# Signals of TensorE carried by a drain behind a batch's last product, in the gather passes of a graph network

## The chip, the cores and the metric

The kernel runs on one core of a Trainium2 chip. The metric is the device time in microseconds of one execution without profiler; the median of 3 executions counts. The engines are TensorE (PE; its weight loads are PEld), VectorE (DVE), ScalarE (ACT), GpSimd (POOL) and SyncE (SP), each with an instruction stream of its own; they wait for each other on semaphores alone.

## What is computed

Four layers of a graph network on 6250 nodes of 64 features and 200000 edges sorted by destination. Each layer normalises the nodes (layer norm, then the positive part), works on the edges and adds its result to the nodes. Cut to the edge work:

```python
def layer0(h): # sum of neighbours
    agg = segment_sum(concatenate([h[src], edge_attr_32], axis=1), dst)
    return relu(concatenate([h, agg], axis=1) @ W.T + b)

def layer1(h): # additive attention; V belongs to the destination
    pre = h[src] @ W_q + b_q + h[dst] @ W_k + b_k + edge_attr_32 @ W_e + b_e
    scores = leaky(pre) @ a_w + a_b
    alpha = segment_softmax(scores, dst)
    return segment_sum(alpha * (h[dst] @ W_v + b_v), dst)

def layer2(h): # weighted sum
    return segment_sum(h[src] * (edge_weight_n2 * edge_weight)[:, None], dst)

def layer3(h): # attention with 4 rules, 8 relations
    q = h[dst] @ Wq + bq
    key = h[src] @ Wk1 + rel_emb[edge_type] @ Wk2 + bk
    scores = ((q * key).sum(-1)[:, None] + q @ key_rule.T) / 8
    mean_attn = segment_softmax(scores, dst).mean(axis=1)
    out = segment_sum(h[src] @ W_r[edge_type] * mean_attn[:, None], dst) + bias
    return relu(layer_norm(out))
```

## The kernel before

Edges are taken in 392 batches of 512, four tiles of 128 edges each. Since edges are sorted, the destinations of one batch lie in a window of 128 nodes, and a segment sum over a batch is a product with one-hot rows of the destination's place in the window.

There are four passes over all batches. Three of them gather rows of a table in HBM by source node, with GpSimd's indirect DMA, one for each tile of 128 edges (`gather_stage`, L785):

- **the sum pass** (`sum_sweep`, layer 0) gathers `node_rows`. In one batch of eight the rows are not gathered but made by TensorE, as products of one-hots with the whole node table in SBUF (`look_up`, L1119); VectorE (L1191) and ScalarE (L1089, L1093) build these one-hots. TensorE's stage `sums` (L1111) makes four products, whose signal s_sum frees the gathered rows and lets VectorE add the sum (L1160).
- **the score pass** (`score_sweep`, layer 1) gathers `src_rows`. TensorE's stage `look` makes one product with the edge features (L1480) and twelve with the table of destination rows (L1485), signal s_looked. VectorE joins them with the gathered rows and computes the scores. ScalarE writes them on the diagonals of four matrices (`spread_stage`, L1391), TensorE's stage `spread` brings them into all partitions (L1382), signal s_spread, and VectorE masks (L1529) and takes the maximum. SP's `stream` waits for s_looked to load the next edge features, ScalarE's spread_stage for s_spread to reuse the diagonals.
- **the attention pass** (`attention_sweep`, layer 3) gathers `rel_rows`. TensorE has four stages: `look` (L1663, twelve products, s_looked), `sum_up` (L1689, four fp32 products, s_sum), `find` (L1680, four small products, s_found), `spread` (L1671 in bf16 and L1382 in fp32, s_spread). VectorE takes the maximum (L1714) and the running maximum in three parts (L1723 to L1756), which `find` waits for; ScalarE makes a factor out of it (`shrinks`, L1629), then the diagonals (L1391), which `spread` waits for.

The fourth pass (`kept_sum_sweep`, layer 2) reads back rows that the score pass has spilled to HBM; nothing is gathered in it.

On each engine `pipeline` (L160) lays the stages out, in one order for every step: a stage with lag n handles in step t the batch t - n. TensorE's orders are `sums`, `lookups` in the sum pass, `look` (1), `spread` (6) in the score pass and `look` (1), `sum_up` (5), `find` (3), `spread` (2) in the attention pass. The steps in the middle are a loop over 8 or 16 unrolled steps. `done(eng, sem, b)` waits until a stage has finished batch b, `free(eng, sem, b, ring)` until the batch that had the same ring slot before is done with it. Gathered rows lie in a ring of 8 batches. GpSimd waits before a batch's gathers for the slot: s_sum in the sum and attention passes, s_pre (VectorE) and the spill in the score pass.

Every one of TensorE's stages signals by an increment on its last product:

```python
for g in range(TILES_PER_BATCH):
    last = pe.matmul(summed, weighted[:, b.slot(2), g, :],
                     rows[:, b.slot(ROW_RING), g, D:2 * D + 1],
                     start=(g == 0), stop=(g == TILES_PER_BATCH - 1))
last.then_inc(s_sum, 1)
```

`look` reads the place of the batch's window out of registers (`dst_table`, `Bases.of`), which is register work of TensorE's own instruction stream. A phase ends in barriers (L215, L218, L221), in which each engine has a drain with a semaphore increment.

Of the kernel before, what the change touches and what calls it, by code (L numbers as in the profile page):

```python
# [64 lines left out]
ROW_RING = 8  # L65
# [172 lines left out]
def graph_layers(nc, a, out):  # L238
    ctx = contextlib.ExitStack()
    with ctx:  # L240
# [689 lines left out]
        def sum_sweep(name):  # L930
# [4 lines left out]
            def sweep():  # L935
                with Phase(nc, name) as ph:
# [163 lines left out]
                    @block.tensor  # L1100
                    def _(pe):
                        def sums(b):
                            done(pe, s_onehot, b)
                            if looked_up(b):
                                pe.wait_ge(s_filled, block_of(b))
                            else:
                                rows_landed(pe, s_rows, b)
                            done(pe, s_joined, b)
                            free(pe, s_added, b, 2)
                            for g in range(TILES_PER_BATCH):  # L1110
                                last = pe.matmul(sum_bank(b), sum_rows[:, b.slot(ROW_RING), g, :],  # L1111
                                                 onehots_of(b)[:, g, :],
                                                 start=(g == 0), stop=(g == TILES_PER_BATCH - 1))
                            last.then_inc(s_sum, 1)

                        def look_up(b, hot, j):
                            for g in range(TILES_PER_BATCH):
                                at = g % 2 * PARTS * D
                                last = pe.matmul(look_banks(b)[g // 2][:, at:at + PARTS * D],  # L1119
                                                 hot[:, g * P:(g + 1) * P], node_parts(j),  # L1120
                                                 start=(j == 0 and g % 2 == 0),
                                                 stop=(j == SRC_TILES - 1 and g % 2 == 1))
                            return last

                        def lookups(b):
                            if not has_lookup(b):
                                return
                            if b.slot(LOOK_EVERY) == 0 and not b.early(2 * LOOK_EVERY):
                                pe.wait_ge(s_filled, block_of(b) - 1)
                            by_dve, by_act = list(hots_dve(b)), list(hots_act(b))  # L1130
                            before_dve, before_act = block_of(b) * HOTS_DVE, block_of(b) * HOTS_ACT
                            for n, m in enumerate(by_dve):
                                pe.wait_ge(s_hot_dve, before_dve + m + 1)
                                look_up(b, dve_hots[:, m % 4, :], m).then_inc(s_used_dve, 1)
                                for k in by_act[n // 2:n // 2 + 1] if n % 2 else []:
                                    pe.wait_ge(s_hot_act, before_act + k + 1)
                                    look_up(b, act_hots[:, k % 2, :], HOTS_DVE + k)\
                                        .then_inc(s_used_act, 1)
                            for k in by_act[len(by_dve) // 2:]:
                                pe.wait_ge(s_hot_act, before_act + k + 1)  # L1140
                                look_up(b, act_hots[:, k % 2, :], HOTS_DVE + k).then_inc(s_used_act, 1)
                        pe.wait_ge(s_parts, (PARTS + 1) * len(src_groups))
                        pipeline(pe, [(0, sums), (0, lookups)], unroll=GATHER_UNROLL)
# [262 lines left out]
        def score_sweep(name):  # L1406


            def sweep():
                with Phase(nc, name) as ph:  # L1410
# [61 lines left out]
                    @block.tensor  # L1472
                    def _(pe):
                        def look(b):
                            parts = dst_table(b)
                            done(pe, s_hot, b)
                            free(pe, s_pre, b, RING)
                            landed(pe, s_dma, b, 16)
                            to = banks[b.slot(RING)][:, 0:TILES_PER_BATCH * D]
                            pe.matmul(to, edge_blocks[:, b.slot(RING), :],  # L1480
                                      w1_e[:, :, :].rearrange("p g f -> p (g f)"),
                                      start=True, stop=False)
                            for g in range(TILES_PER_BATCH):
                                for n, part in enumerate(parts):
                                    last = pe.matmul(  # L1485
                                        to[:, g * D:(g + 1) * D],
                                        onehotT[:, b.slot(ONEHOT_RING), g, :], part, start=False,
                                        stop=(g == TILES_PER_BATCH - 1 and n == PARTS - 1))
                            last.then_inc(s_looked, 1)

                        def spread(b):
                            done(pe, s_diag, b)
                            free(pe, s_max, b, RING)
                            spread_scores(pe, b, spread_bank(b)).then_inc(s_spread, 1)

                        fill_table(pe, w1_k, D, s_table, s_took)
                        pipeline(pe, [(1, look), (6, spread)])
# [87 lines left out]
        def attention_sweep(name):  # L1585
# [3 lines left out]
            def sweep():  # L1589
                with Phase(nc, name) as ph:  # L1590
# [64 lines left out]
                    def _(pe):  # L1655
                        def look(b):
                            parts = dst_table(b)
                            done(pe, s_hot, b)
                            free(pe, s_score, b, RING)
                            for g in range(TILES_PER_BATCH):  # L1660
                                to = banks[b.slot(RING)][:, g * D:(g + 1) * D]
                                for n, part in enumerate(parts):
                                    last = pe.matmul(to, onehotT[:, b.slot(ONEHOT_RING), g, :],  # L1663
                                                     part, start=(n == 0), stop=(n == PARTS - 1))
                            last.then_inc(s_looked, 1)

                        def spread(b):
                            done(pe, s_diag, b)
# [1 line left out]
                            free(pe, s_max, b, 2)  # L1670
                            pe.matmul(spread_bank(b), ident_b[:, :], far3[:, b.slot(2), :],  # L1671
                                      start=True, stop=False)
                            spread_scores(pe, b, spread_bank(b), start=False).then_inc(s_spread, 1)

                        def find(b):

# [2 lines left out]
                            for g in range(TILES_PER_BATCH):  # L1679
                                last = pe.matmul(found[:, g, :], onehotT[:, b.slot(ONEHOT_RING), g, :],  # L1680
                                                 max_parts[:, b.slot(RING), :], start=True, stop=True)
                            last.then_inc(s_found, 1)

                        def sum_up(b):
                            done(pe, s_weighted, b)
# [2 lines left out]
                            for g in range(TILES_PER_BATCH):  # L1688
                                last = pe.matmul(summed, weighted[:, b.slot(2), g, :],  # L1689
                                                 rows[:, b.slot(ROW_RING), g, D:2 * D + 1],  # L1690
                                                 start=(g == 0), stop=(g == TILES_PER_BATCH - 1))
                            last.then_inc(s_sum, 1)
                        fill_table(pe, w3_q, D + N_ACTIVE, s_table, s_took)
                        pe.wait_ge(s_ones, 1)
                        pipeline(pe, [(1, look), (5, sum_up), (3, find), (2, spread)])
# [654 lines left out]
```

## Time and profile before

| | us |
|---|---|
| median of 3 executions without profiler | 6724.05 (6722.16 to 6726.13) |
| the profiled execution (its span, the one time the page gives for it) | 8496.5 |
| busy: PE, PEld | 5207.8, 3779.2 |
| busy: DVE, ACT, POOL | 4828.8, 4212.1, 4954.7 |
| mean granted clock of TensorE, whole span | 0.735 |

The profiled execution took 1772 us longer than one without profiler; durations of instructions come from it. A granted clock of 1.0 is 2.4 GHz for TensorE, 0.5 is 1.2 GHz. "Idle before" is the idle time of an engine ahead of an instruction, and behind "<-" stands what ended it: an instruction, "issue" (nothing that the profile shows) or "remote" (a signal whose sender it does not find). The spans: sum pass to some 2412 us, score pass 2471 to 5112, kept sums 5150 to 5816, attention pass 5921 to 8431.

### The profile page before, as it was taken

To read this page: it belongs to the slowest core of one execution; us is meant where nothing else is said; L and a number is where in the kernel's file an instruction comes from. 1 tells how busy PE (TensorE), PEld (TensorE's weight loads), DVE (VectorE), ACT (ScalarE), POOL (GpSimd) and SP (SyncE) were. 2 spreads that over 40 slices of the span, in tenths; PEclk is the share of its full clock that TensorE was granted. 3 is DMA by queue.
4 is the path that set the end of the run, shared out by engine and by line. 5 is a ranking of instruction groups with operands and counts; after the bars stand their busy time and mean duration, and the time that the engine had idled before them with its cause. 6 is when DMAs were issued, how large, how long until landed. Compare 5 with 4: busy or idle time off the path is not lost. (4 is left out here: it accounts for less than half of the span.)

```text
span 8496.5 us, 161499 instructions
## 1 busy us (share of the span) xinstructions
PE 5207.8 (61%) x38193; PEld 3779.2 (44%) x38194; DVE 4828.8 (57%) x21267; ACT 4212.1 (50%) x11643; POOL 4954.7 (58%) x5713
## 2 busy tenths in 40 slices
PE   4666666666665444444444447998566666666664
PEld 3555555555552222222222226886344444444443
DVE  5545445555545555555555558997555555555556
ACT  3445454455524344334434348995455555555554
POOL 5555555555535555555555556994566666666663
PEclk7888888888876666666666668998676767766666
DMA  4323333233334444444444446886222222222221
GB/s 118 87 80 87 85 86 87 81 84 87 86 83 135 129 128 129 126 129 129 128 126 130 127 127 196 268 267 223 57 63 63 63 63 64 63 62 62 63 64 41
DMA packets 672781, 908.55 MB, mean 107 GB/s; under 512 B 141174, under 2 KB 429928, under 8 KB 672441
## 3 DMA queue, kind: packets, MB, share of 16 engines
q1 hardware_dynamic: 502366, 605.50, 22.8%
q0 software_dynamic: 168944, 301.30, 14.5%
q8 instruction: 42, 0.69, 0.0%
q14 instruction: 72, 0.59, 0.0%
q10 hardware_dynamic: 1357, 0.47, 0.0%
HBM read 696.57 MB, written 210.28 MB: 107 GB/s over the span
## 5 line engine op out<-in xcount | busy, mean ns | idle before, releaser
L785 POOL DMA_INDIRECT rows<-src_rows,idx_slots x1563 | 1495.9, 957 | 1164.2 <-DVE pre L1504 607.0
L785 POOL DMA_INDIRECT rows<-rel_rows,idx_slots x1563 | 1499.3, 959 | 1004.8 <-issue 417.9
L785 POOL DMA_INDIRECT rows<-node_rows,idx_slots x1371 | 1302.9, 950 | 1035.0 <-PE bank L1111 378.9
L1391 ACT ACTIVATE onehot<-ident,fresh_slots 128x128 f32<-128x128 f32 x3136 | 992.6, 387 | 921.8 <-remote 585.7
L1382 PE MATMUL bank<-onehot,ones 128*128 128x512 f32 x1568 | 1315.0, 935 | 6.6 <-ACT onehot L1391 6.6
L1480 PE MATMUL bank<-w_e,edge_in 128*128 128x256 f32 x784 | 429.0, 647 | 1372.4 <-DVE onehots L867 992.1
L1089 ACT ACTIVATE dst_pairs<-pre,minus_node 128x512 bf16<-128x512 int16 x816 | 577.5, 719 | 1173.7 <-remote 807.1
L1480 PEld LDWEIGHTS bank<-w_e,edge_in 128*128 128x128 f32 x784 | 191.3, 294 | 1825.2 <-issue 1195.6
L1119 PE MATMUL bank<-by_chunk,dst_pairs 128*128 128x192 bf16 x6144 | 790.8, 274 | 277.5 <-issue 166.1
L1119 PE MATMUL bank<-wide_room,dst_pairs 128*128 128x192 bf16 x3264 | 489.1, 283 | 559.2 <-ACT dst_pairs L1093 471.0
L1191 DVE TENSOR_SCALAR dst_pairs<-pre,node_at 128x512 bf16<-128x512 int16 x1536 | 545.4, 355 | 493.8 <-remote 332.4
L1529 DVE TENSOR_TENSOR onehots<-bank,onehots 128x512 f32<-128x512 f32 x392 | 269.9, 689 | 892.0 <-remote 605.9
L1119 PEld LDWEIGHTS bank<-by_chunk,dst_pairs 128*128 128x128 bf16 x6144 | 599.0, 110 | 361.5 <-issue 202.1
L1689 PE MATMUL bank<-rows,onehot 128*128 128x65 f32 x3136 | 592.8, 350 | 204.2 <-DVE wide_room L1786 177.9
L1629 ACT ACTIVATE shrink<-grown 128x1 f32<-128x1 f32 x392 | 79.5, 203 | 1150.7 <-DVE grown L1734 747.5
L1689 PEld LDWEIGHTS bank<-rows,onehot 128*128 128x128 f32 x3136 | 546.7, 262 | 224.0 <-issue 203.6
L1463 ACT ACTIVATE onehot<-onehots,exp_bias 128x512 bf16<-128x512 f32 x392 | 282.9, 722 | 684.0 <-DVE max_by_chunk L1561 287.8
L1119 PEld LDWEIGHTS bank<-wide_room,dst_pairs 128*128 128x128 bf16 x3264 | 318.3, 112 | 635.8 <-ACT dst_pairs L1093 512.5
L1093 ACT ACTIVATE dst_pairs<-dst_pairs,ones 128x512 bf16<-128x512 bf16 x816 | 540.8, 707 | 1.6
L1644 ACT ACTIVATE onehot<-onehots,edge_in 128x128 f32<-128x128 bf16 x1568 | 500.5, 389 | 20.0
L1310 ACT ACTIVATE onehot<-onehots,edge_scale 128x128 f32<-128x128 bf16 x1568 | 500.9, 390 | 14.4 <-DVE onehots L1365 14.2
L1160 DVE TENSOR_TENSOR wide_room<-bank,wide_room 96x128 f32 x392 | 112.1, 286 | 658.5 <-PE bank L1111 336.7
(307 smaller groups left out, 12159.5 us busy)
## 6 DMA issues: line engine op xcount, KB each, us to landing
edge_in<-dst_line SPq DMA_DIRECT2D x392, 256.0 KB
spill<-rows SPq DMA_DIRECT2D x392, 256.0 KB
rows<-spill SPq DMA_DIRECT2D x392, 256.0 KB, 3.1
hot_rows<-rows SPq DMA_DIRECT2D x98, 712.0 KB
onehots<-hot_rows SPq DMA_DIRECT2D x196, 356.0 KB, 3.5
onehots<-src_low SPq DMA_DIRECT2D x98, 512.0 KB
edge_in<-in_ea_l SPq DMA_DIRECT2D x98, 256.0 KB
edge_in<-in_eaT_l SPq DMA_DIRECT2D x392, 64.0 KB
```

The lines of the kernel that those rows point to most:

```text
L785: pool.indirect_dma_start(out=to[:, b.slot(ROW_RING), g, :], out_offset=None, in_=table, in_offset=bass.IndirectOffsetOnAxis(ap=idx_slots[ ...
L1089: act.activation(act_hots[:, n % 2, :], look_in(b), ACT.Square, bias=minus_node[:, n:n + 1]).then_inc(s_square, 1)
L1093: act.activation(act_hots[:, n % 2, :], act_hots[:, n % 2, :], ACT.Relu, scale=-1.0, bias=ones[:, 0:1])\
L1119: last = pe.matmul(look_banks(b)[g // 2][:, at:at + PARTS * D], hot[:, g * P:(g + 1) * P], node_parts(j), start=(j == 0 and g % 2 == 0), s ...
L1191: dve.tensor_scalar(dve_hots[:, n % 4, :], look_in(b), node_at[:, n:n + 1], None, ALU.is_equal)\
L1310: last = act.activation(onehot[:, b.slot(RING), g, :], plain_of(b)[:, g, :], ACT.Copy, scale=edge_scale[:, b.slot(RING), g:g + 1])
L1382: return pe.matmul(bank, ones[:, :], diag[:, b.slot(2), :, :].rearrange("p g e -> p (g e)"), start=start, stop=True)
L1391: last = act.activation(diag[:, b.slot(2), g, :], ident[:, :], ACT.Copy, scale=fresh_slots[:, b.slot(2 * RING), g:g + 1])
L1463: act.activation(exp_out, masked1[:, b.slot(2), :], ACT.Exp, bias=exp_bias[:, slot, :], accum_out=exp_sum[:, slot, :])
L1480: pe.matmul(to, edge_blocks[:, b.slot(RING), :], w1_e[:, :, :].rearrange("p g f -> p (g f)"), start=True, stop=False)
L1644: last = act.activation(weighted[:, b.slot(2), g, :], onehot_b[:, b.slot(ONEHOT_RING), g, :], ACT.Copy, scale=share[:, b.slot(RING), g:g + 1])
L1689: last = pe.matmul(summed, weighted[:, b.slot(2), g, :], rows[:, b.slot(ROW_RING), g, D:2 * D + 1], start=(g == 0), stop=(g == TILES_PER_B ...
```

## The change

In the three gather passes the increment moves from the last product of a stage to a drain that TensorE executes behind it. It concerns seven of the nine signals of TensorE in these passes; the signals of the lookups' products (L1119) stay on their products, and so do those of the table fills and of the kept-sum pass. A drain holds TensorE's instruction stream until the engine has finished what was issued. Waits, products, buffers and orders are as before.

```diff
@@ sum_sweep, sums
-                                last = pe.matmul(sum_bank(b), sum_rows[:, b.slot(ROW_RING), g, :],
+                                pe.matmul(sum_bank(b), sum_rows[:, b.slot(ROW_RING), g, :],
                                                  onehots_of(b)[:, g, :],
                                                  start=(g == 0), stop=(g == TILES_PER_BATCH - 1))
-                            last.then_inc(s_sum, 1)
+                            pe.drain().then_inc(s_sum, 1)
@@ score_sweep, look
-                            last.then_inc(s_looked, 1)
+                            pe.drain().then_inc(s_looked, 1)
@@ score_sweep, spread
-                            spread_scores(pe, b, spread_bank(b)).then_inc(s_spread, 1)
+                            spread_scores(pe, b, spread_bank(b))
+                            pe.drain().then_inc(s_spread, 1)
@@ attention_sweep, look
-                            last.then_inc(s_looked, 1)
+                            pe.drain().then_inc(s_looked, 1)
@@ attention_sweep, spread
-                            spread_scores(pe, b, spread_bank(b), start=False).then_inc(s_spread, 1)
+                            spread_scores(pe, b, spread_bank(b), start=False)
+                            pe.drain().then_inc(s_spread, 1)
@@ attention_sweep, find
-                            last.then_inc(s_found, 1)
+                            pe.drain().then_inc(s_found, 1)
@@ attention_sweep, sum_up
-                            last.then_inc(s_sum, 1)
+                            pe.drain().then_inc(s_sum, 1)
```

## Rows read from the trace of the kernel before

**Rows 1.** Three stretches: us, busy us (instructions) of PE, PEld, DVE, ACT, POOL; granted clock; DMA

```profile
58.50:2390.00 2331.50, 1475.92 (x12438) 1309.71 (x12439) 1181.77 (x3202) 1151.06 (x2017) 1301.95 (x1371) 0.81 0.30 85
2471.30:5075.30 2604.00, 1225.85 (x6251) 651.95 (x6251) 1350.78 (x7285) 1013.30 (x3047) 1494.94 (x1563) 0.65 0.46 128
5921.20:8393.10 2471.90, 1629.12 (x10496) 1105.33 (x10496) 1385.29 (x8528) 1255.10 (x4232) 1498.36 (x1562) 0.68 0.24 63
```

**Rows 2.** The gathers' line: count, ns shortest/median/longest, first and last start

```profile
L785 POOL DMA_INDIRECT rows<-rel_rows,idx_slots x1563: 938/944/1357, 5921.2 to 8393.1; - x196
```

**Rows 3.** Timeline of GpSimd, attention pass: start us, us, engine, line

```profile
8349.92 0.94 POOL L785 DMA_INDIRECT rows<-rel_rows,idx_slots  x1 [0.30 <-issue]
8351.17 0.94 POOL L785 DMA_INDIRECT rows<-rel_rows,idx_slots  x1 [0.30 <-issue]
8354.76 0.94 POOL L785 DMA_INDIRECT rows<-rel_rows,idx_slots  x1 [2.65 <-remote]
```

**Rows 4.** Timeline of the score pass around 4007 us

```profile
4007.16 1.10 PE L1382 MATMUL bank<-onehot,ones 128*128 128x512 f32 x2
...
4011.03 0.69 DVE L1529 TENSOR_TENSOR onehots<-bank,onehots 128x512 f32<-128x512 f32 x1 [4.37 <-remote]
```

**Rows 5.** Timeline of the attention pass's tail, clock high

```profile
8397.98 0.39 PE L1671 MATMUL bank<-edge_in,ident_b 128*128 128x512 bf16 x1 [0.28 <-ACT onehot L1391]
8398.21 1.02 PE L1382 MATMUL bank<-onehot,ones 128*128 128x512 f32 x2
8399.07 0.22 PE L1663 MATMUL bank<-by_chunk,onehots 128*128 x2
...
8399.26 0.69 DVE L1714 TENSOR_REDUCE batch_max<-bank 128x1 f32<-128x512 f32 x1
...
8399.41 1.08 PE L1689 MATMUL bank<-rows,onehot 128*128 128x65 f32 x8
...
8402.03 0.39 PE L1671 MATMUL bank<-edge_in,ident_b 128*128 128x512 bf16 x1 [0.28 <-ACT onehot L1391]
```

**Rows 6.** The same tail, TensorE alone, later steps, clock low at first

```profile
8402.25 1.42 PE L1382 MATMUL bank<-onehot,ones 128*128 128x512 f32 x2
...
8404.13 1.95 PE L1689 MATMUL bank<-rows,onehot 128*128 128x65 f32 x8
8406.03 0.27 PE L1680 MATMUL bank<-max_parts,onehots 128*128 128x3 bf16 x4
8406.57 0.61 PE L1671 MATMUL bank<-edge_in,ident_b 128*128 128x512 bf16 x1 [0.27 <-ACT onehot L1391]
8406.97 1.92 PE L1382 MATMUL bank<-onehot,ones 128*128 128x512 f32 x2
8408.67 0.32 PE L1663 MATMUL bank<-by_chunk,onehots 128*128 x2
...
8420.91 1.91 PE L1382 MATMUL bank<-onehot,ones 128*128 128x512 f32 x2
```

**Rows 7.** Busy time and granted clock in the tail

```profile
8393.00:8417.00 24.00, 19.26 (x138) 12.65 (x137) 17.95 (x119) 17.31 (x59) 0.94 (x1) 0.78 0.06 18
```

**Rows 8.** TensorE's last products of the attention pass, and its drain behind them

```profile
8428.74 1.94 PE L1689 MATMUL bank<-rows,onehot 128*128 128x65 f32 x8 [0.63 <-DVE wide_room L1786]
L215 PEldq DRAIN  x1: 1970/1970/1970, 8428.8 to 8428.8; - x1
```

**Rows 9.** Sequencer instructions of TensorE: attention look, and waits anywhere

```profile
L1663 PEldq FUSED_REGOPS  x784: 46/46/51, 5976.6 to 8412.0; - x196
L131 PEldq EVENT_SEMAPHORE  x2312: 51/51/582, 111.1 to 8428.6; - x193
```

**Rows 10.** TensorE from a barrier to the next product: sequencer rows, then the product

```profile
L218 PEldq EVENT_SEMAPHORE  x1: 51/51/51, 5118.7 to 5118.7; - x1
...
L916 PEldq COMPARE_BRANCH  x1: 88/88/88, 5119.0 to 5119.0; - x1
5119.11 1.86 PE L2025 MATMUL bank<-rel_bias,ones 1*1 1x512 f32 x2 [8.00 <-PEq L218]
```

## The prediction

> **What bounds the kernel now.** The three windows that hold the gathers come first: 2331.5, 2604.0 and 2471.9 us, 7407.4 of a span of 8496.5, so 1089.1 us lie outside [rows 1]. In none of them is an engine busy for more than two thirds, which says latency or a wait, not throughput. The same rows count GpSimd's gathers, 1371 + 1563 + 1563 = 4497 (the last one starts on the edge of its window); each is busy 0.94 us [rows 2], and GpSimd's timeline their spacing: 1.25 us from start to start while nothing holds them, then a pause of 2 to 3 us [rows 3]. Nothing but gathers at 1.25 us would take 4497 x 1.25 = 5621 us; with the 1089 us outside, 6710 us. The median without profiler is 6724 us. So I read the plain execution as bound by GpSimd's issue of gathers in all three passes, some 5.0 us a batch (4 x 1.25) in the score and attention passes and 1371 x 1.25 / 392 = 4.4 us in the sum pass, and the profiled execution, 1772 us longer, as one with a disturbance of its own.
>
> What that disturbance is matters here. In the score pass TensorE's last two fp32 spread products, one batch, end by 4007.16 + 1.10 = 4008.26, and those of the batch before have ended earlier; but VectorE, which waits for the signal of a spread, starts its next maximum only at 4011.03, after 4.37 us of idling [rows 4]. Gathers run on meanwhile. In the tail of the attention pass, where the last gather has been issued at 8393.1 [rows 2], VectorE starts 0.03 us behind the product's end (8398.21 + 1.02 = 8399.23, start 8399.26) [rows 5]. So signals carried by products are late while gathers are issued, in the profile. 6710 against 6724 leaves at most 14 us of it without profiler, unless a gather costs less there.
>
> The tail of the attention pass also shows what this pass costs without gathers: the spread's fp32 product starts at 8398.21, and five steps later at 8420.91, so 22.70 us for 5 steps, 4.54 us each [rows 5, 6]. That is less than 0.5 us under GpSimd's 5.0, and the granted clock there is 0.78 [rows 7]; over the whole pass it is 0.68 [rows 1]. The cover is thin in this pass. In the score pass TensorE is busy for 1225.9 / 392 = 3.1 us a batch, in the sum pass for 1475.9 / 392 = 3.8 [rows 1]; there it is wider.
>
> **The change part by part.** It removes seven increments from products and adds seven drains a batch in all: one in the sum pass, two in the score pass, four in the attention pass (look, sum_up, find, spread). 392 x 7 = 2744 drains. No DMA, no queue of SP or GpSimd is touched, no product is moved; but TensorE's own instructions behind a drain now wait for it: the register work and waits of the next group, and its first weight load.
>
> The drain itself: at the end of the attention pass a drain issued at 8428.8 takes 1970 ns, to 8430.7, and the products in front of it end at 8428.74 + 1.94 = 8430.68 [rows 8]. So it ends 0.0 to 0.1 us behind the last product, and holds TensorE's queue all that time. Its signal I bound by 0 and +0.15 us later than a product's 0.03, and take 0.05. It may also be earlier, if the lateness of [rows 4] belongs to products alone; that is a rival below.
>
> The bubble behind it has two parts. (a) The overlap of groups goes: look's first product starts at 8399.07, 0.16 us before the spread ends at 8399.23, cold 0.22 us (8408.67 against 8406.97 + 1.92 = 8408.89) [rows 5, 6]. (b) Register work and waits, done in advance today, come behind the drain. Look has two FUSED_REGOPS of 46 ns a batch (784 / 392), and each group has waits, EVENT_SEMAPHORE of 51 ns [rows 9]. By these durations, with 0.1 for the drain and a wait or two each, the next group starts 0.35 us (look), 0.25 (sum_up), 0.2 (find), 0.2 (spread) behind the end of the one before. By the spacing from instruction to instruction it is more: EVENT_SEMAPHORE at 5118.7, one more instruction, COMPARE_BRANCH at 5119.0, the first product at 5119.11 [rows 10], so 0.4 us for three, 0.13 us each; that makes 0.65, 0.4, 0.3, 0.3. These are my two ends.
>
> A first-principles figure would be lower than both. The Trainium skill, "TensorE: Matmul & The Clock Gate", section "Single matmul latency", has a constant of 183 ns cold and 166 ns warm over the streaming time, an estimate of the whole bubble if only the array had to run empty. By it the attention step, costed as below, would be an estimated 4.05 us at full clock and 5.39 + 4 x 0.18 = 6.1 us at half clock, 4.8 us mixed, under GpSimd's 5.0, and the sum 0. The overlap of 0.16 to 0.22 us in [rows 5, 6] agrees with that constant; part (b) is what it leaves out.
>
> **The attention step, full clock.** Today it is a loop: spread 8397.98 to 8399.23 (1.25 us), VectorE's maximum at 8399.26 and the running values, ScalarE's diagonals, spread again at 8402.03, where TensorE has idled for 0.28 us until ScalarE is done: 4.05 us [rows 5]. Look (8399.07 to 8399.41, and 0.17 that sum_up overlaps: 0.51), sum_up (1.08 us) and find (0.25) lie in the 2.80 us between. With drains TensorE's own order is, from the spread's end: 0.35 + look 0.51 + 0.25 + sum_up 1.08 + 0.2 = 2.39, find 0.25, 0.2, spread 1.25: 4.09 us, nearly all hidden. With the larger bubbles 0.65 + 0.51 + 0.4 + 1.08 + 0.3 + 0.25 + 0.3 + 1.25 = 4.74 us. **Half clock:** spread 2.32 us (8406.57 to 8408.89), look 0.85 (from 8402.25 + 1.42 = 8403.67 to 8404.13, and 0.2 of overlap on either side), sum_up 1.95, find 0.27 [rows 6]; TensorE is then the whole step, some 5.1 us today with an idle of 0.27 for the diagonals. With drains 5.39 of work + 1.0 = 6.39 us, or + 1.65 = 7.04 us. Nothing covers that.
>
> A clock of 0.78 is 56% of time at 2.4 GHz, 44% at 1.2; 0.68 is 36% and 64%. Steps per us add up by shares: today 0.56/4.05 + 0.44/5.1 gives 4.45 us (4.54 measured), with drains 4.86 or 5.54 us; at 0.68, 5.31 or 5.99. The two middles are 5.2 and 5.65. The tail has no stalls of the recording in it, so I count it twice: 5.35 us. Over 5.0 that is 0.35 us x 392 = **+137 us**.
>
> **Sum pass:** one bubble of 0.3 to 0.5 on 3.8 us of TensorE, 4.1 to 4.3 against GpSimd's 4.4: 0, bound +50 us. What covers it are the gathers; without them it would cost 0.3 x 392 = 118 us. **Score pass:** two bubbles, 0.6 to 1.0 on 3.1: 4.1 us under 5.0, cost 0, by the same cover. What is late next in the attention pass is s_sum, which frees the rows that GpSimd gathers into (ring of 8): it evens out single steps, not a mean above 5.0.
>
> The sum is made on the profile's rows and laid on the plain median, since the profiled span, 1772 us longer, has stalls that the plain run can't hold: 6724 + 137 = 6861 us.
>
> **The rivals.** *No change.* GpSimd's 5.0 us covers the drains (step 4.86 or less). For it: the duration rows; against it: the 0.5 us of cover and four drains. 6724 us, up to 6737. It decides where the drained step stays under 5.0 us, that is where bubbles are as short as the durations. The Trainium skill's constant, from the page and section named above, leads to the same result.
>
> *Faster, since signals by a drain aren't late.* If the lateness of [rows 4] is also there without profiler, and gathers are cheaper there than 1.25 us, then 6724 is not GpSimd's bound but late signals, and a drain, which the sequencer carries, could escape it. Its place is every wait for s_looked, s_spread, s_sum; its price at most 4497 x (1.25 - 0.94) = 1394 us, where gathers would follow each other at once; a third of that gives 6260 us. For it: the idling of 4.37 us is large against a step of 5. Against it: 6710 would have to match 6724 by chance. It decides from a plain gather spacing under some 1.2 us.
>
> *The lateness is of the engine, not of the product.* Then a drain's signal is as late, and the change doesn't do what it says; the plain time is as in my forecast or the rival of no change, and its chance lies in theirs.
>
> *More than forecast.* The clock falls further since bubbles thin TensorE's work: 5.99 us a step, +388 us, 7112 us.
>
> **How the numbers follow.** Slower by the attention step: 0.55 (of it 0.07 above 7080). No change: 0.2. Faster: 0.25, most of it far below. The likeliest gives 6861 us. The range takes in no change, most of slower, and a little of faster: 6620 to 7080 us; slower alone has 6740 to 7080. 0.2% (13 us) is what a measurement of this kernel can tell from no change.
>
> **What would show it.** Right: drains of TensorE at the seven places, 392 each; no product overlaps the group before; idle "issue" time in front of look; tail steps of the attention pass of 4.9 to 5.6 us instead of 4.54; fixed part of 1089 us and the kept-sum pass unchanged. Wrong: tail steps under 5.0 (no change), or VectorE's maxima starting behind spread products without the 2 to 4 us of idling, and fewer pauses of GpSimd, in a shorter plain time (the faster rival).

## The result and the profile after

The changed kernel takes 7300.85 us in the median of four executions, the kernel before 6723.11 us in the same comparison. One of the four took 8008 us, at a granted clock of 0.546 over the whole span, the other three 7239.81 to 7310.57 us at 0.71 to 0.72, and the ratio leaves that one out: 1.0827 times as long, 95% interval 1.0808 to 1.0846, some 556 us slower. The forecast was +137 us, 6861 us, with a range up to 7080.

The three stretches that hold the gathers, after the change (us; busy us of PE, PEld, DVE, ACT, POOL; granted clock; DMA), beside [rows 1]:

```profile
58.40:1796.20 1737.80, 1343.58 (x12526) 1207.45 (x12527) 1178.51 (x3222) 1166.00 (x2024) 1320.33 (x1370) 0.90 0.41 116
1874.40:3853.70 1979.30, 1321.59 (x6352) 635.93 (x6352) 1348.21 (x7403) 1010.22 (x3101) 1503.48 (x1562) 0.65 0.64 169
4673.40:7179.60 2506.20, 1986.80 (x10508) 1237.62 (x10507) 1433.47 (x8535) 1256.89 (x4236) 1495.74 (x1562) 0.55 0.24 62
```

Against [rows 1] the first two are shorter by 594 and 625 us, in a kernel that is slower. That is no gain. The profile of before was taken while the chip was in another condition than in the runs that gave 6724 us; what marks the two conditions is shown with the experiments below. The kernel before, profiled where it takes 6717 us (run e7), has these:

```profile
58.20:1794.30 1736.10, 1330.70 (x12527) 1243.03 (x12528) 1174.75 (x3222) 1141.28 (x2024) 1318.51 (x1371) 0.88 0.39 116
1867.00:3840.20 1973.20, 1225.71 (x6350) 606.16 (x6349) 1342.56 (x7401) 1005.82 (x3101) 1497.38 (x1562) 0.69 0.63 169
4659.80:6626.30 1966.50, 1482.08 (x10578) 1012.74 (x10578) 1372.05 (x8598) 1265.75 (x4268) 1486.72 (x1563) 0.78 0.28 79
```

Now nearly all of the difference stands in one place: +1.7 us in the sum pass, +6.1 in the score pass, +539.7 in the attention pass, 5.02 us a batch before and 6.39 after. Of the 26 us that the spans differ by outside the windows (1039.5 against 1066.0 us), 21 lie behind the last gather, in the tail of the same pass; the kept sums take 659 us in both. In the attention window the granted clock fell from 0.78 to 0.55. What GpSimd waits for, from the costliest groups after the change (the releaser and its us last):

```profile
L785 POOL DMA_INDIRECT rows<-rel_rows,idx_slots x1563 | 1496.7, 958 | 1041.7 <-PEq L1694 616.4
L785 POOL DMA_INDIRECT rows<-src_rows,idx_slots x1563 | 1504.5, 963 | 535.8 <-issue 452.7
L785 POOL DMA_INDIRECT rows<-node_rows,idx_slots x1371 | 1321.3, 964 | 422.5 <-issue 411.4
```

In the score and sum passes nearly all of its idle time is "issue", its own spacing. In the attention pass it waits, beyond that, 616.4 us for the drain of sum_up (L1694), which frees the rows. One attention step, TensorE alone:

```profile
6500.00 0.59 PE L1672 MATMUL bank<-edge_in,ident_b 128*128 128x512 bf16 x1 [0.23 <-issue]
6500.38 1.91 PE L1382 MATMUL bank<-onehot,ones 128*128 128x512 f32 x2
6502.72 0.36 PE L1664 MATMUL bank<-by_chunk,onehots 128*128 x2 [0.43 <-issue]
...
6503.41 0.24 PE L1664 MATMUL bank<-wide_room,onehots 128*128 x1
6503.89 1.94 PE L1691 MATMUL bank<-rows,onehot 128*128 128x65 f32 x8 [0.23 <-issue]
6506.06 0.25 PE L1682 MATMUL bank<-max_parts,onehots 128*128 128x3 bf16 x4 [0.23 <-issue]
6506.53 0.59 PE L1672 MATMUL bank<-edge_in,ident_b 128*128 128x512 bf16 x1 [0.23 <-issue]
```

6.53 us from L1672 to L1672, all at half clock, and before each group an idle time ended by "issue": 0.43 + 0.23 + 0.23 + 0.23 = 1.12 us of bubbles. The work is 2.29 (spread) + 0.93 (look) + 1.94 (sum_up) + 0.25 (find) = 5.41 us. No other idle time stands in these rows. The kernel before in the same condition (run e7), two steps:

```profile
6002.88 0.39 PE L1671 MATMUL bank<-edge_in,ident_b 128*128 128x512 bf16 x1 [0.28 <-ACT onehot L1391]
6003.10 1.41 PE L1382 MATMUL bank<-onehot,ones 128*128 128x512 f32 x2
6004.31 0.32 PE L1663 MATMUL bank<-by_chunk,onehots 128*128 x2
...
6005.08 1.94 PE L1689 MATMUL bank<-rows,onehot 128*128 128x65 f32 x8
6007.51 0.27 PE L1680 MATMUL bank<-max_parts,onehots 128*128 128x3 bf16 x4 [0.49 <-DVE max_parts L1756]
6008.01 0.61 PE L1671 MATMUL bank<-edge_in,ident_b 128*128 128x512 bf16 x1 [0.23 <-ACT onehot L1391]
6008.41 1.91 PE L1382 MATMUL bank<-onehot,ones 128*128 128x512 f32 x2
6010.12 0.31 PE L1663 MATMUL bank<-by_chunk,onehots 128*128 x2
...
6013.12 0.61 PE L1671 MATMUL bank<-edge_in,ident_b 128*128 128x512 bf16 x1 [0.18 <-ACT onehot L1391]
```

The second step is at half clock throughout and takes 5.11 us; the first goes over from full to half. Sorted by the length of the spread products at either end of a step (over 1.8 us is half clock, under 1.2 full), the steps of the attention pass's timeline are, before: 23 full, 26 half, 340 between the two, mean 4.98 us. After: none full, 305 of 386 half with a median of 6.54 us, 81 between with a mean of 5.14.

### The profile page after: what moved, and what is told of

Read it like the earlier page. It is cut to its first block and busy times, and to the rows that moved or that the text cites. A ratio compares the mean times of both kernels' runs of the same rounds, so it can differ in the third digit from the quotient of the medians.

```text
span 7289.3 us, 164243 instructions
## 1 busy us (share of the span) xinstructions
PE 5511.6 (76%) x38193; PEld 3780.7 (52%) x38194; DVE 4840.4 (66%) x21267; ACT 4202.2 (58%) x11643; POOL 4979.5 (68%) x5713
## 5 line engine op out<-in xcount | busy, mean ns | idle before, releaser
L785 POOL DMA_INDIRECT rows<-rel_rows,idx_slots x1563 | 1496.7, 958 | 1041.7 <-PEq L1694 616.4
L1382 PE MATMUL bank<-onehot,ones 128*128 128x512 f32 x1568 | 1416.3, 1003 | 99.6 <-issue 66.8
L1480 PE MATMUL bank<-w_e,edge_in 128*128 128x256 f32 x784 | 397.2, 602 | 562.2 <-DVE onehots L867 399.4
L1691 PE MATMUL bank<-rows,onehot 128*128 128x65 f32 x3136 | 696.1, 394 | 104.4 <-issue 102.7
L1119 PE MATMUL bank<-by_chunk,dst_pairs 128*128 128x192 bf16 x6144 | 694.4, 261 | 85.3 <-issue 68.0
L1691 PEld LDWEIGHTS bank<-rows,onehot 128*128 128x128 f32 x3136 | 636.4, 302 | 157.9 <-issue 156.7
L867 DVE TENSOR_TENSOR onehots<-edge_in,window_pair 128x512 bf16<-128x512 int16 x784 | 331.0, 422 | 567.9 <-DMA edge_in<-dst_line 565.1
L1664 PEld LDWEIGHTS bank<-by_chunk,onehots 128*128 128x128 bf16 x3136 | 260.4, 118 | 824.8 <-issue 816.4
L1119 PEld LDWEIGHTS bank<-by_chunk,dst_pairs 128*128 128x128 bf16 x6144 | 537.8, 104 | 178.3 <-DVE dst_pairs L1191 87.8
L1716 DVE TENSOR_REDUCE batch_max<-bank 128x1 f32<-128x512 f32 x392 | 271.2, 692 | 419.3 <-PEq L1675 416.7
L1664 PE MATMUL bank<-by_chunk,onehots 128*128 x3136 | 337.1, 235 | 232.9 <-issue 222.9
```

Source lines behind the costliest of these rows:

```text
L785: pool.indirect_dma_start(out=to[:, b.slot(ROW_RING), g, :], out_offset=None, in_=table, in_offset=bass.IndirectOffsetOnAxis(ap=idx_slots[ ...
L1382: return pe.matmul(bank, ones[:, :], diag[:, b.slot(2), :, :].rearrange("p g e -> p (g e)"), start=start, stop=True)
L1480: pe.matmul(to, edge_blocks[:, b.slot(RING), :], w1_e[:, :, :].rearrange("p g f -> p (g f)"), start=True, stop=False)
L1691: last = pe.matmul(summed, weighted[:, b.slot(2), g, :], rows[:, b.slot(ROW_RING), g, D:2 * D + 1], start=(g == 0), stop=(g == TILES_PER_B ...
```

## The experiments

In what follows "before at" gives the time of the kernel before in the same set of runs. There were seven sets, and the kernel before took 6720 to 6728 us in three of them and 8511 to 8643 in four, with the same code. The first I call the prompt condition of the chip, the second the late one, for a reason that e1 to e4 show.

| run | edit | us | ratio to before, 95% | before at |
|---|---|---|---|---|
| e1 | drains in attention pass only | 8908.75 | 1.0465 (1.0447 to 1.0482) | 8511 |
| e2 | drains in sum and score pass only | 8740.35 | 1.0272 (1.0255 to 1.0289) | 8511 |
| e3 | signal on product, drain behind | 9133.44 | 1.0727 (1.0710 to 1.0745) | 8511 |
| e4 | signal on product, own wait behind | 8838.66 | 1.0392 (1.0368 to 1.0416) | 8511 |
| e5 | the whole change | 7273.59 | 1.0833 (1.0794 to 1.0872) | 6720 |
| e6 | without the drain behind look | 7135.82 | 1.0628 (1.0604 to 1.0652) | 6720 |
| e7 | the kernel before | 6717.08 | one execution | 6725 |
| e8 | as e3 | 7309.27 | 1.0860 (1.0831 to 1.0889) | 6725 |
| e9 | as e1 | 7252.02 | 1.0771 (1.0724 to 1.0818) | 6725 |
| e10 | in the attention pass only spread's drain | 6770.61 | 1.0072 (1.0057 to 1.0087) | 6725 |
| e11 | whole, half of sum_up's products | 8956.07 | 1.0529 (1.0488 to 1.0569) | 8519 |
| e12 | whole, less work in three groups | 8861.91 | 1.0398 (1.0360 to 1.0436) | 8519 |
| e13 | whole, drains of attention pass doubled | 9289.94 | 1.0898 (1.0855 to 1.0940) | 8519 |
| e14 | as e4 | 8885.99 | 1.0434 (1.0392 to 1.0476) | 8519 |
| e15 | as e12 | 9045.38 | 1.0455 (1.0437 to 1.0472) | 8643 |
| e16 | as e4 | 9110.80 | 1.0543 (1.0525 to 1.0560) | 8643 |
| e17 | as e12 | 8876.23 | 1.0428 (1.0404 to 1.0451) | 8511 |
| e18 | as e12 | 6773.49 | 1.0070 (1.0053 to 1.0086) | 6728 |

**Where the loss sits: e1, e2, e9.** Each takes the change back in some passes; in e1 and e9:

```diff
-                            pe.drain().then_inc(s_looked, 1)
+                            last.then_inc(s_looked, 1)
```

(and so for the sum pass's s_sum and the score pass's s_spread); e2 does it at the attention pass's four places.

> Drains at the four places of the attention pass alone; the sum and score passes signal by their products as before. Theory (the attention step is TensorE's own serial order at half clock, 6.5 us a batch, of it 1.1 us in four bubbles): the whole loss, 7250 to 7310 us. Rival (the score and sum passes lose a part too, two bubbles on a latency chain of VectorE): 7100 us or less.

> Drains in the sum pass and the score pass alone; the attention pass as before. Theory (GpSimd's gathers cover three bubbles): 6715 to 6737 us, and in the profile the sum and score windows take about 1738 and 1979 us as with the whole change, while the attention window keeps its long pauses. Rival (these passes lose a part): 6800 us or more.

> Drains in the attention pass alone. Theory (the sum and score passes cost nothing where before takes 6720): 7240 to 7310 us, no less than the whole change. Rival (a part sits in the other passes): under 7200 us.

e9 gives the answer for the prompt condition: the drains of the attention pass alone cost 528 us of the 553 and 585 that e5 and e8 cost in all, and its sum and score windows (1736.8 and 1975.6 us) are those of before. Its attention window:

```profile
4663.50:7120.90 2457.40, 1937.60 (x10498) 1202.96 (x10497) 1430.77 (x8534) 1256.92 (x4236) 1496.34 (x1562) 0.58 0.23 63
```

e1 and e2 met the late condition, in which the expected times mean nothing, but the differences do: +397 and +229 us, and e3, with a drain at all seven places, +622. So there the sum and score passes lose too (the windows of e2 are 2377.7 and 2774.5 us against 2331.5 and 2604.0 in [rows 1]). The expectation for e2 was wrong for that condition. Its timeline shows why, in one step of the score pass:

```profile
3296.38 1.22 PE L1480 MATMUL bank<-w_e,edge_in 128*128 128x256 f32 x2 [1.37 <-issue]
...
3297.99 0.24 PE L1485 MATMUL bank<-wide_room,onehots 128*128 x1
3298.27 0.98 POOL L785 DMA_INDIRECT rows<-src_rows,idx_slots  x1 [1.28 <-issue]
3299.55 0.95 POOL L785 DMA_INDIRECT rows<-src_rows,idx_slots  x1 [0.30 <-issue]
3300.80 0.95 POOL L785 DMA_INDIRECT rows<-src_rows,idx_slots  x1 [0.31 <-issue]
3302.06 0.95 POOL L785 DMA_INDIRECT rows<-src_rows,idx_slots  x1 [0.30 <-issue]
3304.78 2.07 PE L1382 MATMUL bank<-onehot,ones 128*128 128x512 f32 x2 [6.55 <-issue]
```

and the drains of this line, first all 392 of e2, then the four from 3280 to 3306 us, then all of the changed kernel in the prompt condition (ns shortest/median/longest):

```profile
L1489 PEldq DRAIN  x392: 592/2626/12233, 2583.4 to 5320.2; - x196
...
L1489 PEldq DRAIN  x4: 1252/5014/7685, 3276.4 to 3296.8; - x4
```

```profile
L1489 PEldq DRAIN  x392: 590/1432/1680, 1903.2 to 3849.8; - x196
```

Look's last product ends at 3298.23 by its row. The drain behind it, issued at 3296.81, lasts 7.685 us, to 3304.49. GpSimd issues four gathers meanwhile, and the spread starts only when they are over. Sort the 392 drains of this line by whether a gather has started in the 1.3 us before their last product ends. Where one has, 187 of 216 end over 0.3 us late, by 4.5 us in the median; where none has, 11 of 176 do, and the median is 0.02 us. In the changed kernel's own profile, in the prompt condition, it is 2 of 389 with gathers running. So in the late condition the end of look's drain comes late while GpSimd issues gathers. That the same holds for a product's own signal is seen in e4, where TensorE waits on it: from look's last product to the spread's first one passes 4.1 us in the median where a gather is running, 0.13 us where none is (e3, with drains: 4.7 and 0.22). The row of a product does not show this: by the Trainium skill, "Perfetto Trace Analysis", section "Tensor Engine Instruction (MATMUL, LD_WEIGHTS)", the recorded end is computed from the instruction's size, and the semaphore goes once PSUM has acknowledged the last bytes; that the drain, which is recorded itself, ends 6.3 us behind that end agrees with it, and where the time between goes no row shows. What puts the chip into it stays open: two sets on the chip of the same number, at different times, met one condition each.

**Signal or drain: e3 and e8.** The signal stays where it was, the drain comes without one:

```diff
-                            pe.drain().then_inc(s_looked, 1)
+                            last.then_inc(s_looked, 1)
+                            pe.drain()
```

> The signals go back on the last products, and a drain without a signal stands behind each. Theory (the price is the holding up of TensorE's instruction stream, not the place of the signal): as with the whole change, 7250 to 7310 us. Rival (the drain's signal comes late, and those who wait for it make the step): 7000 us or less. Profile: if products' signals are late because of how they are recorded, the pauses in the gather windows come back; if the emptying of TensorE cures it, they stay away.

> Signals on the products and a drain without a signal behind each, this time beside e9 and e10. Theory (what costs is TensorE's instruction stream held up): as the whole change, 7240 to 7310 us where before takes 6720. Rival (the signal's place costs): under 6900 us.

7309.27 us in the prompt condition, within noise the time of the whole change (ratios 1.0860 and 1.0827, their intervals overlap). The place of the signal is worth nothing that can be told from noise; the price is TensorE's instruction stream held up. In the late condition the drains of e3 of the score pass's look end as late as those of e2 (4.5 us in the median with a gather running), and the pauses of the gathers are there, so emptying the engine cures nothing.

**The whole change again, and one drain less: e5, e6.** e6 puts look's signal back on its last product.

> The whole change once more, beside the kernel before. In the first comparison the kernel before took 6723 us; in the four runs above it took 8511 us, as long as its profiled execution of 8496.5, with TensorE's completions late while gathers are issued. Theory (two conditions of the chip that no kernel sets; in the one a completion of TensorE is late, whoever carries it): where before takes 6720 to 6740, the whole change takes about 7300; where before takes 8500, it takes 9080 to 9180, as with a drain behind a signalling product. Rival (a drain cures the lateness): about 7300 us also where before takes 8500.

> The whole change without the drain behind the attention pass's look, whose signal is on its product again. Theory where before takes 6724: one bubble of 0.23 us and nothing else goes from a step of 6.5, 90 us less than the whole change, 7210. Where before takes 8500: the drain behind look is the one that ends late (0.57 us median, 0.67 mean behind its products), so 250 to 350 us less than the whole change. Rival (only the number of drains counts): the same 90 us less in both.

e5 repeats the result (1.0833). e6 takes 138 us off it, more than the 90 expected: its half-clock steps have a median of 6.15 us instead of 6.54. That is 0.39, the bubble of 0.23 and some 0.2 of overlap between look and sum_up that comes back with it.

**How the clock answers: e7, e10.** e10 leaves one drain in the attention pass, the one with the largest bubble.

> The kernel before, for a profile in the condition in which it takes 6720 us (the profile shown of it was taken where it takes 8500). Theory: no pauses of GpSimd; windows of about 1740 us (sum), 1980 (score) and 1930 to 1985 (attention), and in the attention pass a granted clock between 0.68 and 0.8, so that the drains cost through a clock that falls as well as through bubbles. Rival (the clock is 0.55 to 0.6 there already and the bubbles are the whole price): then 392 steps of 6.5 us against 4.95 would need 1.5 us of bubbles, and the profile shows 1.1.

> Of the attention pass's four drains only the one behind spread (those of the sum and score passes stay). It opens the largest bubble, 0.43 us ahead of look, and the largest part of work, 2.3 us at half clock, is ahead of it. Theory (bubbles add up on a serial order of 5.39 us at half clock, and the clock stays high as long as the step fits into 4.95): 5.39 + 0.43 less the overlap that the three products-carried groups keep (0.2 each) = 5.2 us at half clock, about 4.1 at full clock, so 6720 to 6850 us. Rival (the clock falls with any drain): 5.2 to 5.8 us a step all the time, 6800 to 7040 us.

e7 came out as its theory has it. e10's time does too, but not that theory's clock, which was to stay high. The windows of the attention pass, e10 first, then e6 (three drains):

```profile
4669.70:6669.60 1999.90, 1668.05 (x10522) 1045.39 (x10521) 1402.67 (x8548) 1258.16 (x4241) 1500.54 (x1562) 0.67 0.28 77
```

```profile
4667.80:7023.10 2355.30, 1927.37 (x10498) 1226.23 (x10497) 1422.93 (x8534) 1257.14 (x4236) 1494.76 (x1563) 0.55 0.25 66
```

None, one, three and four drains: a clock of 0.78, 0.67, 0.55, and 0.53 to 0.58, in windows of 1966, 2000, 2355 and 2457 to 2536 us. Among the kernels with four drains the window grows as the clock falls: 0.575 and 2457 us (e9), 0.568 and 2472 (e5), 0.552 and 2506 (after), 0.527 and 2536 (e8). One drain costs 46 us only, since its half-clock steps (112 of 386, median 5.36 us) are little above GpSimd's 5.0. Its clock falls all the same, though TensorE is then busier, 83% of the window against 75% in e7. A part of that rise is the clock itself: the same product takes longer at half clock (0.61 us against 0.39 for the bf16 one of spread in e7), so a busy share can't be read as the cause of a clock. What changed is that TensorE now stands empty ahead of groups that it used to overlap; why the clock answers to that isn't shown.

**What makes the bubble: e13, and e4, e14, e16.** e13 puts a second drain, without signal, ahead of each of the attention pass's four. e4 and its repetitions replace the drain:

```diff
-                            pe.drain().then_inc(s_looked, 1)
+                            last.then_inc(s_looked, 1)
+                            done(pe, s_looked, b)
```

> The whole change, with a second drain without signal ahead of each of the attention pass's four. Theory (a bubble is emptying plus instructions issued one after the other behind it; the second drain finds the engine empty and adds its own issue only, some 0.05 to 0.1 us, four times a step): 0.2 to 0.4 us a step, 7360 to 7460 us. Rival (a drain has a fixed price of its own, that of a whole bubble of 0.28 us): 1.1 us a step, 7700 us.

> No drain: the signals are on the last products, and TensorE then waits on its own signal before it goes on. Theory (emptying the engine costs, however it is asked for): a step of 6.4 to 6.9 us, 7200 to 7450 us. Rival (the drain instruction itself costs): 6724 to 6900 us.

> As e4: signals on the last products and no drains, but TensorE waits for its own signal before it goes on. Theory where before takes 6720 (emptying the engine costs, however it is asked for): 7200 to 7350 us. Rival (the drain instruction itself costs): 6900 us or less.

> The kernel of e4 and e14 again. Theory, where before takes 6720 (emptying the engine costs, however it is asked for): 7150 to 7350 us. Rival (the drain instruction itself costs): 6900 us or less. In the other condition it was 250 to 300 us under a drain behind a signalling product, so a part of a drain's price there may be its own.

All four met the late condition. The two drains of spread in e13:

```profile
L1676 PEldq DRAIN  x392: 1825/2292/2337, 6245.1 to 9226.6; - x196
...
L1677 PEldq DRAIN  x392: 13/13/13, 6247.5 to 9228.9; - x196
```

The second takes 13 ns and ends 0.08 us (median) behind the first, and look starts 0.41 us behind it, as it does behind a single drain. So a drain that finds the engine empty adds 0.08 us, 4 x 0.08 x 392 = 125 us a run; e13 has a ratio 1.7% above that of e3, some 145 us. e3 was in another set of runs, so that agreement is a rough one. The rest of a bubble lies behind the drain, in waits, register work and the start of the next products, which these rows don't part. With the own wait the kernel loses 4 to 5% too, so emptying costs without any drain instruction. The size of that in the prompt condition wasn't obtained. Where e4 loses less than e3 is seen in the gaps of the attention pass: from look to sum_up 0.28 us in the median in e4, 0.77 in e3, from find to spread 0.06 against 0.21; its score window is 132 us shorter and its attention window 154 us. e14 repeats these gaps, but e16, in another set of runs, has 0.77 us from look to sum_up as e3 has, so whether a drain has a price of its own there stays open.

**Is it TensorE's serial time against the gathers? e11, e12, e15, e17, e18.** All seven drains stay; work goes:

```diff
-                            for g in range(TILES_PER_BATCH):
+                            for g in range(2):
```

in sum_up (e11), and in the others also spread's bf16 product (L1672) and two of look's three products per tile. These kernels leave out work that the result needs; they serve the time alone.

> The whole change, with two of sum_up's four products left out. Theory (where before takes 6720, the step is TensorE's serial order at half clock, 6.53 us for 305 of 386 steps): these steps lose 0.97 us and take 5.56, still above GpSimd's 5.02, so about 6950 us, at a granted clock of 0.55 to 0.65 in the attention pass. Rival (the drains cost by what the receivers of the signals wait): sum_up's length takes no part in it, 7200 us or more.

> As e11_half_sum_up, and also without spread's bf16 product (0.61 us at half clock) and with one of look's three products per tile (0.57 us less). All four drains stay. Theory: the drained order is 5.39 - 0.97 - 0.61 - 0.57 + 1.12 = 4.36 us at half clock, under GpSimd's 5.02, and the drains cost nothing: 6710 to 6750 us, although the clock is low. Rival (a drain costs whatever TensorE's load is): 6850 us or more.

> The kernel of e12 again (two of sum_up's products, spread's bf16 product and two of look's three products per tile left out), since that set of runs fell into the condition with late completions. Theory, where before takes 6720: 4.36 us of drained order at half clock, under GpSimd's 5.02: 6710 to 6750 us. Rival (a drain costs whatever TensorE's load is): 6850 us or more.

> The kernel of e12 and e15 once more, since both fell into the condition with late completions (before at 8519 and 8643 us). Theory, where before takes 6720: 4.36 us of drained order at half clock, under GpSimd's 5.02: 6710 to 6750 us. Rival (a drain costs whatever TensorE's load is): 6850 us or more.

> The kernel of e12, e15 and e17 a last time. Theory, where before takes 6720: 4.36 us of drained order at half clock, under GpSimd's 5.02: 6710 to 6750 us. Rival (a drain costs whatever TensorE's load is): 6850 us or more. Where before takes 8500 or more, nothing new is expected: 1.04 times before, as in the three runs so far.

Only e18 met the prompt condition, so only it decides; in the late one the time goes by the held-up completions (e12: 2598 us of attention pass with the short order too), and e11's own question was not answered. e18, the attention window and then one step:

```profile
4675.30:6677.50 2002.20, 1479.19 (x5491) 733.72 (x5490) 1396.55 (x8542) 1257.39 (x4239) 1514.96 (x1563) 0.50 0.30 77
```

```profile
5503.47 2.05 PE L1382 MATMUL bank<-onehot,ones 128*128 128x512 f32 x2 [0.23 <-ACT onehot L1391]
5505.94 0.39 PE L1664 MATMUL bank<-by_chunk,onehots 128*128 x4 [0.43 <-issue]
5506.56 1.08 PE L1689 MATMUL bank<-rows,onehot 128*128 128x65 f32 x4 [0.23 <-issue]
5507.88 0.25 PE L1680 MATMUL bank<-max_parts,onehots 128*128 128x3 bf16 x4 [0.23 <-issue]
5508.36 2.05 PE L1382 MATMUL bank<-onehot,ones 128*128 128x512 f32 x2 [0.23 <-ACT onehot L1391]
```

The clock is at half, 0.50, all the time, all bubbles are there at their full size, and the loss is 46 us (1.0070) where the whole change loses some 556. That is the theory's case: what costs is the order of TensorE above the 5.0 us of four gathers. The forecast of 6710 to 6750 was missed by 23 us, since the order takes 4.89 us and not 4.36 (the median step is 4.97 us): the spread's fp32 products take 2.05 us when no bf16 product runs ahead of them, and sum_up's two 1.08. A cover of 0.1 us lets single waits through (window +36 us over e7).

## Why the prediction was wrong

**What bounds the kernel.** Right. In the prompt condition GpSimd's gathers are the bound in all three passes, 5.02 us a batch in the attention pass (1966.5 / 392). That the sum of 6710 us came so near to 6724 is luck in part: in e7 the three windows take 5676 us and not 5621, and 1040 us lie outside them and not 1089. And the long profiled execution was put down to the recording. It was the late condition, which the kernel before meets without profiler too (8511 us), so [rows 4] and what stands around it are those of another condition.

**Sum and score passes at 0.** Right, +1.7 and +6.1 us.

**The bubbles.** Right, near the low end: 0.43, 0.23, 0.23, 0.23, together 1.12, with 1.0 and 1.65 given. The drain ends 0.02 us behind its products, 0.0 to 0.1 given. The half-clock step is 6.53 us, 6.39 to 7.04 given; the full-clock step shows once, at the end of the window, in these rows,

```profile
7177.50 0.38 PE L1672 MATMUL bank<-edge_in,ident_b 128*128 128x512 bf16 x1 [0.23 <-issue]
...
7181.86 0.38 PE L1672 MATMUL bank<-edge_in,ident_b 128*128 128x512 bf16 x1 [0.23 <-issue]
7188.06 0.59 PE L1672 MATMUL bank<-edge_in,ident_b 128*128 128x512 bf16 x1 [0.23 <-issue]
7194.59 0.59 PE L1672 MATMUL bank<-edge_in,ident_b 128*128 128x512 bf16 x1 [0.23 <-issue]
...
7212.99 0.59 PE L1672 MATMUL bank<-edge_in,ident_b 128*128 128x512 bf16 x1 [0.23 <-ACT onehot L1391]
```

as the 4.36 us between the first two, with 4.09 to 4.74 given. The Trainium skill, "TensorE: Matmul & The Clock Gate", section "Single matmul latency", gives a constant of 183 ns for a product on its own at the low clock. With that for each bubble the half-clock step was an estimated 6.1 us, short by 0.4; three of the four bubbles are 0.05 us above it, the one ahead of look, with its register work, 0.25.

**The step that failed** is "a clock of 0.78 is 56% of time at 2.4 GHz, 44% at 1.2; 0.68 is 36% and 64%", both of before, put under the drained steps (0.68, besides, is the late condition's; e7 has 0.78). The clock didn't stay: with the drains it fell to 0.55, 10% of time at 2.4 GHz. With 10% and 90%, my own step values give 1 / (0.1/4.09 + 0.9/6.39) = 6.05 us at the low end and 6.71 at the high one. The measured steps of 4.36 and 6.53 give 6.22 us, (6.22 - 5.0) x 392 = +478 us; with the old share of 56% they would give 5.11 us, +43. So the term that was mis-sized is the clock's share, and by this working it carried some 435 us of the loss. What is left between 6.22 and the measured 6.39 us a batch, some 65 us, the sum doesn't hold: half-clock steps have a median of 6.54 us but a mean of 6.75. It is a working and not a measurement, as no run has four drains at the old clock. Nor would the fallen clock alone do it: the steps of before, some 4.2 us at full and 5.1 at half clock in e7, come to an estimated 5.0 us at the new share, which is GpSimd's. The two work together: with the bubbles the clock falls (0.78, 0.67 and 0.55 in e7, e10 and e6), and at the low clock the drained order takes 6.5 us instead of 4.4, where 5.0 are free.

**The rivals.** "More than forecast: the clock falls further" is what happened, and its 7112 us was still short, as it stopped at 0.68. Of my 0.55 for slower only 0.07 lay above 7080 us. Faster by timely signals: in the prompt condition there are next to no late ones (2 of 389 drains of the score pass's look with a gather running), and in the late one a drain's completion is no earlier than a product's; the remark that the lateness is the engine's and not the product's was right. No change would have needed a step under 5.0; e18 shows that case, with less work.

**The signs named ahead.** Drains at seven places, 392 each, no overlap of groups, "issue" in front of look: seen. Tail steps of 4.9 to 5.6 us: not seen, five of them take (7212.99 - 7181.86) / 5 = 6.23 us, the last of them without a look. Kept-sum pass unchanged: seen. Fixed part of 1089 us: 1066, against 1040 in e7. VectorE's maxima without the long idling: seen, but in the kernel before of e7 as well, hence no sign of the change.

## What to carry to other kernels

Where TensorE's serial order at half clock is already above the bound of another engine, price a bubble at the half-clock step, not at the mix of clocks of today: here 1.1 us of bubbles cost 1.4 us a step, since the clock fell with them. A drain behind a group of products costs some 0.2 to 0.4 us of empty TensorE and gives the signal no earlier; leave the increment on the last product. Where the order fits under the other engine's bound even at half clock (e18), the same bubbles cost next to nothing. And compare a profile's span with the plain times before using its waits; a gap of 26% was another condition of the chip.

## What the runs showed of the hardware that was not expected

- The same kernel takes 6720 or 8511 us (8643 in one set), steady within a set of runs. In the late condition TensorE's completions are late while GpSimd issues gathers, by 4.5 us in the median of e2's look in the score pass. It strikes the sum pass's sums, look in both passes, and the attention pass's sum_up where a gather is running; the 392 drains behind the score pass's spread, in the same run, end 0.02 us behind their products in the median. Why some groups and not others stays open.
- The granted clock of TensorE fell although its busy share, which slower products raise by themselves, rose or stayed: 0.78 at 75% busy (e7), 0.67 at 83% (e10), 0.55 at 79% (after), 0.50 at 74% (e18, with less work). Its cause isn't shown.
- A drain on an empty TensorE takes 13 ns and 0.08 us from end to end (e13).
